# A four-layer graph network on one core: last-pass norms in pairs, their squares summed on ScalarE, their scaling partly on GpSimd, and other placements

## The reference, cut to what matters

```
x = layernorm(x + layer(x, adj))        # over the 64 channels, eps 1e-5
```

```
v = x with node 0 replaced
for _ in range(3):
    effects = adj @ v
    h = relu([v, effects] @ W1.T + b1)
    v = h @ W2.T + b2
x = layernorm(x + v)
```

## Time and profile before

| what | us |
|---|---|
| three runs | 1100.78, 1098.0, 1098.6 (median 1098.6) |
| the profiled execution's own time | 1096.39 |
| its span, first to last instruction | 1094.6 |
| TensorE busy | 1032.6 (94%) |
| VectorE busy | 781.2 (71%) |
| GpSimd busy | 456.2 (42%) |
| ScalarE busy | 406.6 (37%) |
| mean granted TensorE clock | 0.986 of 2.4 GHz |

### The profile page before, as it was taken

One profiled execution on the slowest core, in us unless ns is written; L12 is line 12 of the kernel. 1 busy time (PEld: TensorE's weight loads), 2 busy tenths in 40 slices (PEclk: granted clock), 3 DMA queues, 4 the chain that ended last, 5 costly groups with the idle time before them and its releaser, 6 DMA issues.

```text
span 1094.6 us, 18614 instructions
## 1 busy us (share of the span) xinstructions
PE 1032.6 (94%) x6922; PEld 494.2 (45%) x6922; DVE 781.2 (71%) x1887; ACT 406.6 (37%) x878; POOL 456.2 (42%) x543
## 2 busy tenths in 40 slices
PE   6989999999999999999999999999999999995993
PEld 2446444434443433334355555555545445552442
DVE  5855676778658876887776877785576867678556
ACT  3632233333334344444424644653445221221211
POOL 0003597546357766885662503443252322222000
PEclk9999999999999999999999999999999999998897
DMA  9750000000000000000010221112112000000111
GB/s 370 258 230 1 1 2 1 1 1 1 1 1 2 1 1 2 1 1 2 1 40 1 78 78 40 66 51 77 65 52 77 1 2 1 3 20 29 30 30 49
DMA packets 14657, 45.65 MB, mean 42 GB/s; under 512 B 960, under 2 KB 9280, under 8 KB 10080
## 3 DMA queue, kind: packets, MB, share of 16 engines
q1 hardware_dynamic: 14560, 44.39, 11.0%
HBM read 40.19 MB, written 4.19 MB: 41 GB/s over the span
## 4 chain that ended last, share of the span: by engine, by line
PE 73%; DVE 14%; POOL 3%; ACT 3%; issue 3%; DMA 2%; SPq 0%; DVEq 0%; ACTq 0%; POOLq 0%
PE PS L713 32%; PE PS L842 17%; PE PS L886 15%; DMA R<-at_in 2%; DVE X L1146 2%; DVE T L1146 2%; PE PS L699 1%; PE PS L700 1%; PE PS L698 1%; POOL X L1697 1%; ACT T L1005 1%; POOL T L1697 1%; DVE R L1146 1%; DVE T L1149 1%; DVE BW L1143 1%
## 5 line engine op out<-in xcount | busy, mean ns | idle before, releaser
L713 PE MATMUL PS<-BW,S 128*128 128x512 fp8e4 x1792 | 405.0, 380 | 8.1 <-DVE R L1146 4.0
L713 PEld LDWEIGHTS PS<-BW,S 128*128 128x128 f16 x1792 | 170.0, 98 | 216.1 <-issue 17.8
L842 PE MATMUL PS<-WZ,R 64*128 64x512 f16 x1536 | 198.9, 377 | 3.2 <-ACT T L1005 3.2
L1005 ACT ACTIVATE T<-PS,SM 128x128 f32<-128x128 f32 x384 | 112.8, 366 | 201.2 <-DVE X L1146 131.0
L1697 POOL TENSOR_TENSOR T<-T 128x128 f32<-128x128 f32 (+1 forms) x192 | 131.0, 682 | 120.5 <-ACT T L1005 109.6
L1146 DVE SCALAR_TENSOR_TENSOR X<-PS,SM,X 128x128 f32<-128x128 f32 x320 | 109.6, 342 | 28.2 <-PE PS L842 27.2
L886 PE MATMUL PS<-BW,S 128*128 128x512 fp8e4 x512 | 117.7, 384 | 10.8 <-DVE X L1146 10.3
L842 PEld LDWEIGHTS PS<-WZ,R 64*128 64x128 f16 x1536 | 69.0, 94 | 107.4 <-issue 25.4
L1697 POOL TENSOR_TENSOR S<-R,S 128x512 f16<-128x512 f32 x48 | 58.1, 1223 | 122.0 <-ACT S L1005 122.0
L842 PE MATMUL PS<-WZ,T 64*128 64x512 f16 x768 | 103.8, 376 | 0.0
L1697 POOL TENSOR_TENSOR T<-R,T 128x512 f16<-128x512 f32 x36 | 42.5, 1181 | 141.2 <-DVE T L1138 80.8
(11 more groups left out here) (214 smaller groups left out, 1434.4 us busy)
## 6 DMA issues: line engine op xcount, KB each, us to landing
WZ<-a_in SPq DMA_DIRECT2D x16, 1024.0 KB, 4.8
R<-at_in SPq DMA_DIRECT2D x15, 1024.0 KB, 6.2
out<-X SPq DMA_DIRECT2D x16, 256.0 KB, 2.3
X<-x_in SPq DMA_DIRECT2D x3, 1024.0 KB, 14.3
T<-w_in SPq DMA_DIRECT2D x1, 1536.0 KB, 9.5
R<-at_in SPq DMA_DIRECT2D x2, 512.0 KB, 4.8
SM<-sm_in SPq DMA_DIRECT2D x1, 520.5 KB, 15.8
X<-x_in SPq DMA_DIRECT2D x2, 256.0 KB, 4.5
```

The source lines that it names most:

```text
L713: m = e.matmul(o, stile(h, t, c), Bm[:, t, block(j)], start=(t == 0 and h == 0), stop=(last and t == NT - 1 and h == 1))
L842: m = e.matmul(bank(b0 + q), halves[kd][zh][r, :], WZ[r, wh, kd, block(g)], start=(i == 0), stop=(i == 8))
L1005: return e.activation(o, i, f, **kw)
```

## The change

- In the last pass `F` and `sq` of a unit stand where a table puts them: those of slots 4 to 6 of round 6 move from half slots 38 to 43 to 41 to 45, the others stay. The last unit but one's `sq`, `var3`, `rs3` move from between the halves of half slot 55 to behind it.
- `var3` and `rs3` take the two units of a slot at once (16 columns, not 8), except for the last two units, and come later (36, 43, 46, 47, 49, 54 and 56).
- The squares of the first 14 units are summed by ScalarE: eight activations of 64 columns, each with an accumulated output, in place of one of 512 columns and VectorE's reduction.
- `out` of ten units (the eight of round 6 and the two of slot 5 in round 7) goes to GpSimd.
- The low half of slot 6's result goes from VectorE to GpSimd in rounds 4, 5 and 6.
- From the second half of slot 4 of a round on, only banks 6 and 7 are lent.
- `gcol` and `step` come one half slot later, as do `total` and `verdict`; the second `fin` too.
- `bt`: none in units 4, 5, 8 and 9, two a round in units 12 to 15; 64 in all as before.

```diff
@@ -135,7 +136,10 @@
-            order += [("Z", u, t), ("add", u, t), ("bt", 4 * u + t)]
+            order += [("Z", u, t), ("add", u, t)]
+            for _ in range(2 if u >= 12 else u < 4 or j >= 2):
+                order.append(("bt", mask_sums))
+                mask_sums += 1
@@ -194,8 +198,7 @@
-        on(h + 1, ("gcol", p, g), ("step", p, g))
-        on(h + 2, *take(n, 0, "X11"))
+        on(h + 2, ("gcol", p, g), ("step", p, g), *take(n, 0, "X11"))
@@ -211,24 +214,23 @@
-    on(15, ("total",))
-    on(16, ("verdict",))
+    on(16, ("total",))
+    on(17, ("verdict",))
...
+
+    for n, s, jj, h in ((6, 1, 0, 33), (6, 1, 1, 34), (6, 4, 0, 41), (6, 4, 1, 42), (6, 5, 0, 43), (6, 5, 1, 44), (6, 6, 0, 44),
+                        (6, 6, 1, 45), (7, 1, 0, 47), (7, 1, 1, 48), (7, 4, 0, 52), (7, 4, 1, 53), (7, 5, 0, 54), (7, 5, 1, 55)):
+        on(h, ("F", *ending(n, s, jj)), ("sq", 3, *ending(n, s, jj)))
+    for n, s, h in ((6, 1, 36), (6, 4, 43), (6, 5, 46), (6, 6, 47), (7, 1, 49), (7, 4, 54), (7, 5, 56)):
+        u = ending(n, s, 0)
+        on(h, ("var3", *u, 2), ("rs3", *u, 2), ("out", *u), ("out", *ending(n, s, 1)))
+    u, v = ending(7, 6, 0), ending(7, 6, 1)
+    between[55] = [("F", *u)]
+    w = half[56]
+    half[56] = [("sq", 3, *u), *w[:2], ("F", *v), ("sq", 3, *v), ("var3", *u, 1), ("rs3", *u, 1), *w[2:], ("out", *u),
+                ("var3", *v, 1), ("rs3", *v, 1), ("out", *v)]
...
-        n, h = 6 + g, 14 * (2 + g)
-        on(h + 1, ("fin", g))
-        for s in ENDS:
-            for jj in range(2):
-                u, e = ending(n, s, jj), h + 2 * s + jj
-                first, then = [("F", *u), ("sq", 3, *u), ("var3", *u)], [("rs3", *u), ("out", *u)]
-                if e == 54:
-                    between[55] = first
-                    on(56, *then)
-                elif e == 55:
-                    on(56, *first, *then)
-                else:
-                    on(e + 2, *first)
-                    on(e + 3, *then)
+        on((29, 44)[g], ("fin", g))
@@ -545,6 +547,8 @@
+                        elif s == 4 and q == 2:
+                            banks = (6, 7)
@@ -605,7 +609,7 @@
-            return (3, *x[1:]) if x[0][-1] == "3" else x[1:]
+            return (3, *x[1:3]) if x[0][-1] == "3" else x[1:]
@@ -613,7 +617,8 @@
-                    SQN[x[1:]] = held[buf] = len(SQN)
+                    SQN[x[1:]] = len(SQN)
+                    held[buf] = x[1:]
@@ -621,13 +626,28 @@
+        REDN = {x: n for n, x in enumerate(y for y in SQN if y[0] < 3 or not order3(*y[1:]) < 14)}
+        ORDER3 = [ending(n, s, jj) for n in (6, 7) for s in ENDS for jj in range(2)]
+
+        def first_of(c, j):
+
+            return (3, c, j) if (3, c, j) in VARN else (3, c, j - 1)
+
+        def by_gpsimd(c, j):
+
+            return order3(c, j) < 8 or order3(c, j) in (12, 13)
+
+        def summed_by_act(c, j):
+
+            return order3(c, j) < 14
+
...
-        def st_part(L, c, j, k):
+        def st_part(L, c, j, k, m=1):
...
-                return ST[:, 2 + order3(c, j) % 2, k, 0:8]
+                return ST[:, 2 + order3(c, j) // 2 % 2, k, 8 * (j % 2):8 * (j % 2) + 8 * m]
@@ -1040,13 +1060,27 @@
-                    if SQPREV[L, c, j] is not None:
-                        e.wait_ge(s_red, SQPREV[L, c, j] + 1)
+                    if L == 3 and summed_by_act(c, j):
+                        r = order3(c, j) // 2
+                        if r >= 2:
+                            e.wait_ge(s_rs, RSN[first_of(*ORDER3[2 * r - 4])] + 1)
+                            e.wait_ge(s_sq, SQN[L, c, j])
+                        o, q = four(sq_buf(L, c, j)), st_part(L, c, j, 0)
+                        for i in range(8):
+                            t, d = i // 2, slice(64 * (i % 2), 64 * (i % 2) + 64)
+                            m = fn(o[:, t, d], X[:, 4 * j + t, 128 * c + d.start:128 * c + d.stop], ACT.Square, accum_out=q[:, i:i + 1])
+                        m.then_inc(s_sq, 1)
+                        continue
+                    if L == 3:
+                        e.wait_ge(s_sq, SQN[L, c, j])
+                    elif SQPREV[L, c, j] is not None:
+                        e.wait_ge(s_red, REDN[SQPREV[L, c, j]] + 1)
...
+                    m = step[3] if L == 3 else 1
...
-                    fn(st_part(L, c, j, 1), st_part(L, c, j, 2), ACT.Sqrt).then_inc(s_sd, 1)
+                    fn(st_part(L, c, j, 1, m), st_part(L, c, j, 2, m), ACT.Sqrt).then_inc(s_sd, 1)
@@ -1151,6 +1185,12 @@
+
+        def scaled(e, c, j):
+
+            v = xpart(c, j).rearrange("p t (b o) -> p t b o", o=C)
+            r = st_part(3, c, j, 2).rearrange("p (t b) -> p t b", b=2).unsqueeze(3).broadcast_to([128, 4, 2, C])
+            return e.tensor_tensor(v, v, r, ALU.mult)
@@ -1404,12 +1444,14 @@
+                    if L == 3 and summed_by_act(c, j):
+                        continue
...
-                    e.wait_ge(s_red, SQN[L, c, 3] + 1)
+                    e.wait_ge(s_red, REDN[L, c, 3] + 1)
@@ -1417,15 +1459,18 @@
-                    c, j = step[1:]
-                    u = order3(c, j)
-                    e.wait_ge(s_red, SQN[3, c, j] + 1)
-                    e.wait_ge(*((s_n[1], 16) if u < 2 else (s_n[3], u - 1)))
-                    ts(e, st_part(3, c, j, 2), st_part(3, c, j, 0), 1 / 64, 1e-5 * 4096, ALU.mult, ALU.add).then_inc(s_var, 1)
+                    c, j, m = step[1:]
+                    if summed_by_act(c, j):
+                        e.wait_ge(s_sq, SQN[3, c, j + m - 1] + 1)
+                    else:
+                        e.wait_ge(s_red, REDN[3, c, j] + 1)
+                    r = order3(c, j) // 2
+                    e.wait_ge(*((s_n[1], 16) if r < 2 else (s_n[3], 2 * r - 2)))
+                    ts(e, st_part(3, c, j, 2, m), st_part(3, c, j, 0, m), 1 / 64, 1e-5 * 4096, ALU.mult, ALU.add).then_inc(s_var, 1)
...
-                    s0, s1, s2 = (st_part(L, c, j, k) for k in range(3))
+                    s0, s1, s2 = (st_part(L, c, j, k, step[3] if L == 3 else 1) for k in range(3))
@@ -1486,6 +1531,8 @@
+                    if s == 6 and n < 7:
+                        continue
@@ -1611,12 +1658,11 @@
-                elif kind == "out":
+                elif kind == "out" and not by_gpsimd(*step[1:]):
...
-                    e.wait_ge(s_rs, RSN[3, c, j] + 1)
-                    v = xpart(c, j).rearrange("p t (b o) -> p t b o", o=C)
-                    r = st_part(3, c, j, 2).rearrange("p (t b) -> p t b", b=2).unsqueeze(3).broadcast_to([128, 4, 2, C])
-                    e.tensor_tensor(v, v, r, ALU.mult).then_inc(s_n[3], 1)
+                    e.wait_ge(s_rs, RSN[first_of(c, j)] + 1)
+                    e.wait_ge(s_n[3], order3(c, j))
+                    scaled(e, c, j).then_inc(s_n[3], 1)
@@ -1761,6 +1807,18 @@
+                elif kind == "V" and step[1] < 7 and step[2] == 6:
+                    n, s, jj = step[1:]
+                    k = place(n // 2, *ending(n, s, jj))
+                    c, j = ending(n, s, jj)
+                    e.wait_ge(s_gh, k + 1)
+                    e.wait_ge(s_gl, k)
+                    add(T[:, c, 1, block(j)], RT[rt_buf(s, jj)], T[:, c, 0, block(j)], ALU.subtract).then_inc(s_gl, 1)
+                elif kind == "out" and by_gpsimd(*step[1:]):
+                    c, j = step[1:]
+                    e.wait_ge(s_rs, RSN[first_of(c, j)] + 1)
+                    e.wait_ge(s_n[3], order3(c, j))
+                    scaled(e, c, j).then_inc(s_n[3], 1)
```

More of the change, by code:

```diff
@@ L119, in middle_order @@
     order = []
+    mask_sums = 0
     for k in range(5):
```

## The result

The changed kernel takes 1074.1 us (median of 4 runs, 1072.7 to 1074.9); the kernel before took 1098.4 us beside it (4 runs, 1098.0 to 1100.8). The ratio is 0.9773, with a 95% interval of 0.9756 to 0.979: faster by 2.3%. The profiled execution took 1074.16 us, span 1072.4, against 1096.39 before: 22.2 us less, where the sum of the prediction had 27.2.

A forecast was written before the change was run, and what follows sets the result against it. TensorE, busy 94% of the span, was taken as the bound, with time only in its gaps. Terms 17.4 + 3.1 + 3.2 + 3.5 = 27.2 us off 1096.39, plus 2.2 for the median, gave 1071.4 us; range 1066 to 1084.

The forecast's parts named there:

- the likeliest case: The prediction's own case, all four terms holding: 1071.4 us, by its bounds 1067 to 1076; chance 0.62.
- the middle: Last pass, TensorE's waits for the low half (5.1 us), for bank 0 (10.3) and lower clock (1.96) go: 17.4 us.
- `gcol` and `total`: Placing `gcol` and `total` behind one more product hides gaps of 1.1, 0.9 and 1.1 us: 3.1 us.
- the tail: From half slot 55 to the last scaling: end at 1088.7 against 1091.9, a gain of 3.2 us.
- product 42: Sign: the product of half slot 42 in the last pass should take 3.6 us, at the higher clock.
- the gap inside 55: Sign: TensorE's gap ahead of the `F` inside half slot 55 stays at about 2 us, moved, not gone.
- `bt`: Fewer `bt` gain 4.3 us in units 5, 8 and 9, 16 more in 12 to 15 cost 0.8: 3.5 us.
- Nothing is left to hide there: Claim for the last pass: the removed waits have no successor, TensorE is the bound again, all 17.4 us go.
- the first rival: ScalarE's sums dear (3.6 us a unit), tail gains only 0.6, `bt` gains nothing: 1077.5 us; chance 0.20.
- GpSimd takes back what it is given: GpSimd's scalings and low halves may hold VectorE up to 20.7 us, undoing part of its relief: 1081.8 us; chance 0.07.
- The change doesn't reach the wait: The wait at 1014.64 is for something other than the bank, so 10.3 + 2.0 us stay: 1083.7; chance 0.06.
- ScalarE in the way: Sums add 41.6 us to ScalarE's queue ahead of evacuations in rounds 6 and 7: up to 1113 us, slower; chance 0.03.

## Why the prediction was right, and where not

**Right in sign and near in size.** 1074.1 us lies within the range and inside the likeliest case's own. Three of the four terms held, a little above forecast: the middle 17.9 (17.4 forecast), `gcol` and `total` 3.7 (3.1), the tail 3.6 (3.2). Of the signs named ahead, product 42 takes 3.62 us, no gap over 1 stands between 930 and half slot 55, the gap inside 55 is 1.86 (2.0), the activations take 242 ns (260) with 112 reads, and the last scaling ends 10.6 us behind the last product (11).

**The step that failed is `bt`: forecast at 3.5 us, worth nothing.** The prediction said of units 12 to 15: "VectorE idles before most of its reductions there, which absorbs most; I charge 0.8", and added 4.3 for units 5, 8 and 9. Both halves came out otherwise. An average of idle time was used where one place decides: at the turn from unit 12 to 13 a root and four `apply` follow the `bt` without a pause, the second `bt` made a gap of 2.07 us there, one of 0.81 came elsewhere, and the lower clock behind the first cost 1.7 (it fell so in four of the six traces with this gap). And the gaps in units 5, 8 and 9 shrank by 2.5 us and not by 4.3. VectorE is done with the reduction sooner, but TensorE, which has waited less before, is there almost as much sooner. In the run with the squares on VectorE, where the clock is full up to there, the reduction's gap in unit 9 ends 2.4 us earlier behind the gap of unit 3 than with `bt` spread, and begins 1.9 earlier.

That the doubling is at fault for the new gap is shown by moving just those 16: 4.7 us of the body come back. Against one `bt` a round the new placement is a draw in the timed runs, and 0.7 us worse in the body with the clock taken out.

The part up to 681 went 3.0 us the wrong way instead of 3.5 the right way. Of these 6.5 us about 3.95 are the gaps (0.45 more instead of 3.5 fewer) and 1.7 the clock behind the new gap; the 1.7 at 231 and the 0.75 gained ahead of it are the profiled execution's luck, bad and good, and no fault of a term. 6.5 less 1.5 that the other terms brought above forecast is the 5.0 us by which the sum is off. The timed median lies nearer, 2.7 us above the forecast.

One sum was a little off: the prediction took 0.27 us for an activation with its read, though 0.26 and 0.19 less two overlaps of 0.1 give 0.25; it measured 0.24.

**Right in sum, but redundant in its parts.** "Nothing is left to hide there" was true of all edits of the middle together (17.9 us against 17.4). The split of this sum was not right. The prediction put 10.3 us down to the bank, by a releaser that the lending alone indeed removes; but that run gained 6.9 of the body, not 12.3 (the wait and the clock's 2.0). And without the lending the change is as fast. With the old norms the waits for the bank and for the low half come from one backlog of VectorE, which shows at whatever waits for it. Banks and places alone are not enough (ratio 0.9909). Beside the lighter norms the later `F` is worth some 6 us in the timed runs, 4.0 of them seen as waits, and the lending nothing that can be measured. Of the lighter norms, ScalarE's sums and GpSimd's scalings are each dispensable. That one of them must stay was not tried, and the pairs and the low half of slot 6 on GpSimd were never taken out alone, so their share is not shown.

**The rivals.** "`bt` a draw" was half of the first rival, and that half happened; the other, dear sums, did not (1.9 us a unit against its 3.6). *GpSimd takes back what it is given* did not happen in the change: its scalings take 1.04 us, less than the 1.36 assumed, TensorE has no gap from 960 to 1050, and taking them away gained nothing (the body is 1.3 us longer, one execution each). The Trainium skill, "GPSIMD Engine Reference", section Engine selection, would keep elementwise work on VectorE, as GpSimd is about twice as slow. The rows of the kernel after agree that it is slower, by half rather than by double (1042 against 692 ns for the same scaling), and the run shows that this did not decide. *The change doesn't reach the wait* and *ScalarE in the way* fell with the timeline of the change. But with `F` at its old places both helpers did hold TensorE up (1.45 and 2.56 us), so the two rivals were kept off by the later `F`, a condition that the prediction does not name where it prices the two.

**Open.** Why the clock falls behind some gaps and not behind others of the same length; 2 of the 6 us of the earlier `F`; and whether the old places would do with the squares left on VectorE.

## What to carry to other kernels

Where one engine's in-order queue feeds another through several waits, add up its work in the whole stretch before pricing the waits one by one: removing one wait shows the next, and an edit that looks decisive alone may be worth nothing beside the others. The total does not settle it: with 53 us of VectorE's work in 90 TensorE still waited, for work handed to other engines whose result was wanted too soon. Give such work a later use along with the new engine. When work is moved out of a crowded place, judge the place it goes to by its worst block without a pause, not by the idle time on average; a pass further on there may be room at no cost. A wait of TensorE can cost more than its length through the clock: here one of 2.07 us was followed by a loss of 1.7 more.

## What the runs showed of the hardware

- **Clock behind short gaps.** TensorE's gap of 2.33 us at 231 is in 13 of the 14 traces. In eight of them, that of the kernel before among these, the granted clock stays 1.00 behind it; in five, the change among them, part of the next 10 us runs at the lower level (0.66 over 5 us in the change), which cost 1.7 us. Behind the gap of 2.07 at 484 it did so in four traces of the six that have it, and behind the one of 2.12 in unit 9 in two of five. Behind the gaps of 1.63 us and less in units 4 to 15 it stayed full in all.
- **Accumulated squares.** A 64-column activation with its read costs 0.24 us from start to start, though the two last 0.24 and 0.19 in the profile.
- **GpSimd.** An in-place product of 128x512 numbers with a broadcast factor took 1.04 us on it, against the 1.36 of its additions that the prediction went by the earlier trace rows; on VectorE it took 0.69. The four `apply` of VectorE at the turn from unit 12 to 13 took 4.23 us in the six traces with the doubled `bt` and 3.41 or 3.42 in the eight others. GpSimd was busy beside them in both (3.97 of the 4.23, 3.19 of the 3.42), at different operations, so what lengthened them is not shown.
